# The second expert stage's front taken apart: its lists built in the attention's last steps, its late groups judged inside the expert loop

## The reference

```python
x = x + 0.5 * ffn(layernorm(x))      # stage 1
x = x + attention(layernorm(x))      # 16 heads of 64, causal, rotary
x = x + 0.5 * ffn(layernorm(x))      # stage 2, the same weights

def ffn(x):                          # per token, 8 experts, the best 2
    logits = x @ router.T            # 8 values
    top_vals, top_idx = top_k(logits, 2);  shares = softmax(top_vals)
    out = sum over the two e of  share_e * ( (silu(x @ gate[e].T) * (x @ up[e].T)) @ down[e].T )
```

## Time and profile before

| | us |
|---|---|
| runs shown (3): lowest, median, highest | 1264.59, 1265.62, 1267.65 |
| the profiled execution, its own time | 1263.21 |
| its span, first to last instruction | 1261.5 |
| TensorE busy (matmuls) | 1196.3, 95% |
| VectorE busy | 905.5, 72% |
| ScalarE busy | 791.4, 63% |
| GpSimd busy | 814.1, 65% |

### The profile page before, as it was taken

How to read it: one execution, slowest core, us unless ns; L and a number is a source line. 1 busy time by engine, 2 the same in 40 slices (tenths; PEclk the granted TensorE clock), 3 DMA queues, 4 the chain that set the end, 5 groups by cost and what they waited for, 6 DMA issues and landing times. The chain is left out here.

```text
span 1261.5 us, 28429 instructions
## 1 busy us (share of the span) xinstructions
PE 1196.3 (95%) x8838; PEld 912.5 (72%) x8838; DVE 905.5 (72%) x1995; ACT 791.4 (63%) x2264; POOL 814.1 (65%) x888
## 2 busy tenths in 40 slices
PE   7799999979999999999999999999999879999992
PEld 6588888856667666666667667766666668888881
DVE  6775344468888888888888997798998767533543
ACT  4665665656667666667667667767666656555552
POOL 4233356259888788788787787677666437666662
PEclk8899999989999999999999999999999969999996
DMA  9135122122221222122212222211221051113223
GB/s 323 32 96 155 57 56 70 42 69 56 62 53 42 60 60 50 44 60 54 57 46 51 62 64 51 60 43 43 52 49 37 18 184 43 47 50 113 62 63 110
DMA packets 87758, 86.54 MB, mean 69 GB/s; under 512 B 11248, under 2 KB 78704, under 8 KB 87232
## 3 DMA queue, kind: packets, MB, share of 16 engines
q1 hardware_dynamic: 76640, 65.50, 20.1%
q0 software_dynamic: 8864, 18.17, 5.2%
q10 hardware_dynamic: 2112, 1.05, 0.3%
HBM read 33.43 MB, written 17.69 MB: 41 GB/s over the span
## 5 line engine op out<-in xcount | busy, mean ns | idle before, releaser
L1915 POOL TENSOR_SCALAR at_prob<-at_prob,at_rec 128x128 f32<-128x128 f32 (+3 forms) x256 | 311.8, 1223 | 154.2 <-DVE at_rec L2126 152.3
L2306 ACT ACTIVATE at_prob<-at_s,at_nb 128x128 f32<-128x128 f32 (+3 forms) x512 | 264.7, 535 | 16.8 <-DVE at_nb L2118 13.4
L2317 ACT ACTIVATE at_probT<-at_pt 128x128 f32<-128x128 f32 (+3 forms) x256 | 105.2, 437 | 223.5 <-PE at_pt L2022 223.1
L790 POOL DMA_INDIRECT f_xb<-xn_dram,f_source x142 | 141.2, 994 | 160.4 <-PE f_b L1285 100.3
L2118 DVE TENSOR_REDUCE at_nb<-at_s 128x2 f32<-128x256 f32 (+3 forms) x256 | 203.5, 816 | 7.8 <-PE at_s L2008 7.8
L1447 DVE TENSOR_TENSOR f_hid<-f_b,f_silu 128x512 f32<-128x512 f32 x142 | 98.5, 693 | 135.8 <-PE f_b L1298 99.6
L2022 PE MATMUL at_pt<-ident,at_prob 128*128 128x128 f32 x1280 | 183.1, 275 | 5.5 <-DVE at_probT L2140 1.6
L2112 DVE TENSOR_TENSOR at_turned<-at_pj,rope 128x1024 f32<-128x1024 f32 x122 | 148.9, 1220 | 44.7 <-PE at_pj L1969 41.7
L2003 PE MATMUL at_s<-at_KT,at_QT 64*128 64x128 f32 (+3 forms) x1024 | 175.2, 460 | 5.2 <-DMA at_KT<-at_probT 2.8
L1909 POOL TENSOR_TENSOR at_R<-at_turned 128x512 f32<-128x512 f32 x126 | 157.4, 1268 | 24.0 <-DVE at_turned L2112 24.0
L2022 PEld LDWEIGHTS at_pt<-ident,at_prob 128*128 128x128 f32 x1280 | 140.9, 141 | 26.9 <-issue 15.5
(11 more groups left out here) (326 smaller groups left out, 2220.1 us busy)
## 6 DMA issues: line engine op xcount, KB each, us to landing
at_QT<-at_R SPq DMA_DIRECT2D x128, 128.0 KB, 2.4
at_KT<-at_R SPq DMA_DIRECT2D x124, 128.0 KB, 2.4
ys_dram<-y SPq DMA_DIRECT2D x71, 64.0 KB, 1.7
f_down<-down_t SPq DMA_DIRECT2D x2, 2048.0 KB, 9.3
xn_dram<-f_xn SPq DMA_DIRECT2D x12, 256.0 KB, 6.7
f_xb<-xn_dram,f_source POOLq DMA_INDIRECT x142, 2.5
X<-x SPq DMA_DIRECT2D x4, 512.0 KB, 6.2
gate<-gate_t SPq DMA_DIRECT2D x8, 256.0 KB, 5.1
```

What stands on the lines that cost most here:

```text
L790: pool.indirect_dma_start(out=xb[j % AHEAD][:, :], out_offset=None, in_=xn_dram, in_offset=bass.IndirectOffsetOnAxis(ap=routing.source[:, ...
L1915: pool.tensor_scalar(w, w, rec[:, q, 1:2], None, ALU.mult).then_inc(probB_ready, 1)
L2306: act.activation(prob[q][:, h, :], s_bank[q % 2][:, h, 0:n], ACT.Exp, bias=nb[:, q, h:h + 1], scale=1.0, accum_out=sums[:, q, h:h + 1]).th ...
L2317: act.activation(probT[0][:, 0:q + 1, q * P:(q + 1) * P], pt_bank[0][:, at:at + (q + 1) * P].rearrange("p (b r) -> p b r", r=P), ACT.Copy) ...
```

## The change

`Lead` gets the tiles for the leading lists (`place_lists`) in the space of `w_hi` and `w_lo`, and the four gather buffers with them. The attention's steps then build the leading lists: `blocked` at the end of VectorE's step 61, two `spots` each at the end of steps 62 and 63, `numbered` on GpSimd behind its step 62, `token_numbered` at the end of ScalarE's steps 62 and 63, `find` in TensorE's step 64 between `out_project` and the last `turn_probs`, `take_found` and `sources` at the end of VectorE's step 64. GpSimd issues the first four gathers behind its last step, in the attention's block. The front's block is gone. Its loads and stores stand at the head of the loop's block on SP, up and down first; groups 4 to 6 are normalised at the head of the loop and turned and judged in step 0 ahead of `project(0)`; the last group is normalised in step 0 and turned and judged in steps 2 to 4; its factors come from VectorE alone, without the square root, in step 0. `targets` of the leading part moves to step 1, and the late tiles' sorting starts at step 4 instead of 0 and ends at 22 instead of 20.

```diff
@@ Lead @@
+        self.routing.place_lists(room)
+        self.xb = [room(f"xb{k}", [P, P]) for k in range(self.AHEAD)]
...
+    def gather(self, pool, j):
+        routing, sure = self.routing, self.routing.sure
+        pool.wait_ge(routing.lists_ready, routing.SOURCES[j >= sure])
+        if j in (0, sure):
+            pool.wait_ge(self.xn_out, 16 * (self.NB // 4 if j else self.LEAD // 4))
...
@@ ffn @@
-            if lead is not None:
-                LATE_GROUPS = range(LEAD_GROUPS, GROUPS)
-                with nc.Block() as block:
...
-        COUNT_AT = 3
-        FIND_AT = 12
+        CHOOSE_AT, COUNT_AT, PLACE_AT, DIGITS_AT, FIND_AT = (4, 7, 10, 10, 14) if lead else (0, 3, 6, 7, 12)
+        BLOCKED_AT = DIGITS_AT + 1
+        SPOTS_AT = BLOCKED_AT + 2
...
@@ ffn, sync @@
+                    sp.dma_start(up[1][:, :, :].bitcast(F32), up_lo_dram).then_inc(up_lo_moved, 16)
+                    sp.dma_start(down[:, :, :, :], down_t).then_inc(down_in, 16)
+                    for g in LATE_GROUPS:
+                        sp.wait_ge(xn_ready, g + 1)
+                        if g < LAST:
+                            sp.wait_ge(xn_ready_pool, g - LEAD_GROUPS + 1)
+                        sp.dma_start(xn_dram[4 * g * P:4 * (g + 1) * P, :].rearrange("(n p) d -> p n d", p=P),
+                                     late_xn[:, 4 * g - LEAD:4 * g + 4 - LEAD, :]).then_inc(xn_out, 16)
...
@@ ffn, gpsimd @@
-                for j in range(AHEAD):
-                    gather(pool, j)
+                if lead:
+                    for g in range(LEAD_GROUPS, LAST):
+                        for n in (4 * g + 2, 4 * g + 3):
+                            one = pool.tensor_scalar(late_xn[:, n - LEAD, :], X[:, n, :], rstd[:, n:n + 1],
+                                                     lead.shift[:, n:n + 1], ALU.mult, ALU.add)
+                        one.then_inc(xn_ready_pool, 1)
...
@@ ffn, tensor @@
-                    if SPLITS and j == 0:
-                        pe.wait_ge(w_lo_dve, 4)
+                    if j == 0:
+                        if SPLITS:
+                            pe.wait_ge(w_lo_dve, 4)
+                        else:
+                            pe.wait_ge(up_lo_moved, 16)
...
+                        if lead and j == 0:
+                            late_turn(LEAD_GROUPS)
+                            late_turn(LEAD_GROUPS + 1)
+                            late_judge(LEAD_GROUPS)
+                            late_turn(LEAD_GROUPS + 2)
+                            late_judge(LEAD_GROUPS + 1)
+                            late_judge(LEAD_GROUPS + 2)
                         if has(j, -2):
                             turn_hidden(j - 2, k)
+                        if lead and j in LAST_TURNED:
+                            last_turn(j)
+                        if lead and j in LAST_JUDGED:
+                            last_judge(j)
...
@@ ffn, scalar @@
                 routing.odds(act, 0, exp_ready)
+                if lead:
+                    late_normed(LEAD_GROUPS)
+                    late_normed(LEAD_GROUPS + 1)
                 for j in range(-1, BLOCKS + 3):
+                    if lead and j == 0:
+                        late_taken(LEAD_GROUPS)
+                        late_normed(LEAD_GROUPS + 2)
+                        late_taken(LEAD_GROUPS + 1)
+                        late_taken(LEAD_GROUPS + 2)
...
                     step(act, j, j % AHEAD)
+                    if lead and j == 0:
+                        late_normed(LAST)
...
@@ ffn, vector @@
-                    routing.targets(dve, 0)
+                    for n in range(NB - 4, NB):
+                        dve.bn_stats(stats[:, n, :], X[:, n, :]).then_inc(moments.stats_ready, 1)
...
                 for j in range(-1, BLOCKS + 3):
+                    if lead and j == 0:
+                        some = slice(NB - 4, NB)
+                        dve.wait_ge(moments.stats_ready, NB)
+                        variances(link, dve, some, stats, mean, rstd, tmpa, tmpb)
+                        guess(link, dve, some, mean, rstd, tmpa)
+                        for _ in range(3):
+                            refine(link, dve, some, rstd, tmpa, tmpb)
...
@@ attention @@
+        LEAD_BLOCKED = STEPS - 3
+        LEAD_FOUND = STEPS
+        found_bank = s_bank[0][:, 0, 0:2 * routing.most]
...
@@ attention, gpsimd @@
                         normalise_b(i, 2)
+                    if i == LEAD_BLOCKED + 1:
+                        for k in range(2):
+                            routing.numbered(pool, 0, k, lead.lead_numbered)
+                for j in range(lead.AHEAD):
+                    lead.gather(pool, j)
...
@@ attention, tensor @@
                         out_project(i - 2)
+                    if i == LEAD_FOUND:
+                        pe.wait_ge(exp_ready, 8 * STEPS)
+                        pe.wait_ge(lead.lead_numbered, 2)
+                        for c in range(4):
+                            routing.find(pe, 0, c, found_bank)
...
@@ attention, vector, lead_last @@
+                    if i == LEAD_BLOCKED:
+                        routing.blocked(dve, 0, 0)
+                        routing.blocked(dve, 0, 1)
+                    if i in (LEAD_BLOCKED + 1, LEAD_BLOCKED + 2):
+                        for c in range(2):
+                            routing.spots(dve, 0, 2 * (i - LEAD_BLOCKED - 1) + c)
+                    if i == LEAD_FOUND:
+                        routing.take_found(dve, 0, found_bank)
+                        routing.sources(dve, 0)
                     if i == REST_FACTORS:
                         lead.halves(dve, 1)
...
@@ attention, scalar @@
-                act.activation(lead.tmpb[:, 0:1], lead.tmpa[:, 0:1], ACT.Sqrt)
+                    if i in (LEAD_BLOCKED + 1, LEAD_BLOCKED + 2):
+                        routing.token_numbered(act, 0, i - LEAD_BLOCKED - 1)
```

More of the change, by code:

```diff
@@ L340, in open, with place_later @@
         self.spot = sb("spot", [P, BLOCKS])
[L341 removed]
+    def place_later(self, sb):
+        self.counts = sb("counts", [P, 2, self.E * self.n[1]])
+        self.past = sb("past", [P, (self.blocks - self.sure + 6) * 3 * self.E])
     def hits_of(self, dve, r, k, logits):
@@ L637, in pack, with __init__, __call__ @@
                 one.then_inc(self.lists_ready, 1)
+class Room:
+    def __init__(self, nc, name, first, stop):
+        self.nc, self.name, self.first, self.stop = nc, name, first, stop
+    def __call__(self, name, shape, dt=F32):
+        size = math.prod(shape[1:]) * (2 if dt == BF16 else 4)
+        tile = self.nc.alloc_sbuf_tensor_at(f"{self.name}_{name}", shape, dt, offset=self.first)
+        self.first += -(-size // 32) * 32
+        assert self.first <= self.stop
+        return tile
 class Lead:
-    def __init__(self, nc, ctx, X, xn_dram, router_t, ident, stats, mean, rstd, tmpa, tmpb, wts, const, NB, E):
+    AHEAD = 4
+    def __init__(self, nc, ctx, X, xn_dram, router_t, ident, stats, mean, rstd, tmpa, tmpb, wts, const, NB, E, room):
         def sem(n):
@@ L1105, in ffn @@
         gate_bank, up_bank, hid_bank, x_bank, y_bank = bank[0:2], bank[2:4], bank[4:6], bank[6], bank[7]
+        if lead:
+            LATE_GROUPS = range(LEAD_GROUPS, GROUPS)
+            LAST = GROUPS - 1
+            late_xn = sb("late_xn", [P, NB - LEAD, P], ctx=work)
+            late_xts = [sb(f"late_xts{k}", [P, 512], ctx=work) for k in range(2)]
+            late_logits = hid_bank[1][:, 0:(NB - 4 - LEAD) * E]
+            last_xts = late_xts[LAST % 2]
+            last_logits = x_bank[:, 2 * P:2 * P + 4 * E]
+            late_turned, late_judged = lead.xt_psum, lead.lg_psum
+            LAST_TURNED = {2: range(0, 3), 3: range(3, 4)}
+            LAST_JUDGED = {3: range(0, 3), 4: range(3, 4)}
         xt_psum = sem("xt_psum2")
@@ L1261, in gather_back @@
                     ).then_inc(odd_in if b else first_in[m // 2], 16)
-                for j in range(AHEAD):
-                    gather(pool, j)
+                if lead:
+                    for g in range(LEAD_GROUPS, LAST):
[3 more added lines that the diff above has]
+                        one.then_inc(xn_ready_pool, 1)
+                else:
+                    for j in range(AHEAD):
+                        gather(pool, j)
                 for j in range(BLOCKS + 3):
```

242 lines of the change are left out of this document (115 added, 127 removed).

## The result

The changed kernel takes 1271.78 us (median; 1267.63 to 1272.7) where the kernel before takes 1265.37 (1264.59 to 1267.65): a ratio of 1.0042, 95% interval 1.0029 to 1.0056. It is slower, by more than the noise, and outside the forecast range (1259.8 to 1270.2). The profiled execution took 1271.77 us with a span of 1270.0, 8.5 us above the span of before.

A forecast was written before the change was run, and what follows sets the result against it. TensorE was taken to bound the kernel, so only its waits, lower clock or reduced work pay. Head −10.35, attention's tail +8.6 and loop +1.4 summed to −0.35: 1265.3 us for the median, range 1259.8 to 1270.2.

The forecast's parts named there:

- head: From the block's start to project(0): 19.55 us become 9.2, −10.35; up's landing gives the lower bound, 8.6.
- (a): End of VectorE's step 61: two block rows, 2 × 0.80 us, against 0.85 idle: +0.75.
- (b): End of VectorE's step 62: two spot tiles, 2 × 1.22 us, against 1.29 idle: +1.15.
- (c): End of VectorE's step 63: two more spot tiles, 2.44 us against no idle, delaying what queues behind: +2.4.
- (d, g): find's 32 matmuls between out_project(62) and the last turn, +1.5, and TensorE's clock falling at find, +1.1.
- (e): Attention's end: source list and four gathers, 6.0 us, against the old chain's 5.94; block ends with the later: +0.3.
- (f): Two GpSimd products beside VectorE delay the normalisation before a maximum of step 63: +1.4, bounds 0 and 3.05.
- loop: TensorE, never idle there, pays for the last group's four transposes and 8 judging matmuls: +1.4.
- exclusive lock: Rival: inserts wait for GpSimd normalisations begun before them, both products come between VectorE's instructions: +5.0, 1270.3 us; chance 0.08.
- up waits for down: Rival at project(0): up lands only when down has too, after 14.3 us: +5.4, 1270.7 us; chance 0.1.

The follow-up runs named there:

- The two runs on the gathers: Against the changed kernel: all four gathers moved into the loop's block, 1267.51 us; only gather 0 left at the attention's end, 1268.04 us.
- the run with the extra turns: Changed kernel plus unread turns of the identity in TensorE's waits in step 63 and ahead of out_project(62): 1267.37 us, ratio 1.0005.
- the second traces of both kernels: Both kernels run again untouched for another trace each: the changed one 1270.35 us, the one before 1265.22 us.

## Why the prediction was wrong

Term by term, forecast and measured:

| term | forecast | measured |
|---|---|---|
| head | −10.35 | −9.98 |
| (a) blocked, step 61 | +0.75 | +0.73 |
| (b) spots, step 62 | +1.15 | +1.34 |
| (c) spots, step 63 | +2.4 | +2.39 |
| (d, g) find, and the clock at it | +2.6 | +2.72 |
| (e) lists and gathers against the old end | +0.3 | +4.46 |
| (f) products beside VectorE | +1.4 | +1.82 |
| clock in step 63 | none | +1.45 |
| loop | +1.4 | −0.6 |
| ahead of the change | none | +4.15 |

(a) is the 0.92 of the table above less 0.19, which the attention lost between the two maxima and which two traces of before differ by as well (0.17). (b) and (f) share 3.16: the two held operations took 1.19 and 1.15, and 0.17 and 0.35 in the kernel before, which makes 1.82; the rest is put down to the spots.

**The failed step is (e): "The block ends with the later: +0.3".** The forecast let the attention's block end when the last gather instruction had ended, and laid the hand-over of an ordinary block behind it. The two runs on the gathers show a block's end that waits 4.3 to 4.6 us behind GpSimd's last gather, and that is gone when the gather stands elsewhere. The trace of before had a row for it that I did not look for, since I looked only at the ends of the attention and of the front, where GpSimd had nothing in flight: at the end of the expert loop the last scatter ends at 1239.65, and the next block's first load stands at 1244.49, 4.84 us later. With that row (e) would have been +4.6. What the sentence says of the engines did come true: the last gather ended at 1026.58, 0.41 behind the residual's end at 1026.17. The block just does not end there.

**(f) and the clock in step 63** are one mis-sized mechanism with a tail. The price was within its bounds (0 to 3.05), but what was held up were not normalisations: it was two operations of 0.17 us each, until the end of the product beside them. I read the first pair of the earlier trace rows as a VectorE operation that takes twice as long; by the two operations here it is rather one that waits. The Trainium skill (SBUF — State Buffer, section "SBUF: two separate sides") has whoever starts first, a GpSimd operation or a VectorE operation of certain kinds, hold the shared pair for its whole instruction. For a GpSimd product with two inputs the run with the products on VectorE agrees (1.19 becomes 0.16). For GpSimd's normalisation with one input the changed kernel agrees no more than the second pair of the earlier trace rows: begun at 996.24, it was drawn out to 2.52 by spot tiles that began after it. So the rival "exclusive lock" was half right, and the doubt that I drew from one pair was good for that kind of instruction only. Spot tiles and hold together left TensorE without work from 1000 to 1002, and its clock fell there a first time, which the forecast had only at find; the run with the extra turns shows 1.56 for it. The hold alone is not to blame: with the products on VectorE the clock falls there too.

**The loss ahead of the change** was no term, because nothing there was edited. It comes and goes: by 1.4 us between two traces of the kernel before, by 3.6 between traces of the changed kernel's code. The 4.15 are those of two single traces, of which the one before was quick (1263.21 against a median of 1265.37); of the 6.41 us between the medians the rests explain 4.4 to 4.5, which leaves about 2 for it. Without it the sum would be +4.4 against the forecast −0.35: inside the range, but still off by (e).

**What held:** the head, its bound by up's landing (project(0) waited 0.37 us for it), and its lower clock; that down comes forward at no price (the rival "up waits for down" is out: up landed after 9.3 us with down right behind it); the sizes of (a) to (d). In the second traces of both kernels the head measures −10.65 (19.49 us become 8.84, with up landed after 8.1). **The loop** was dearer in its first steps, as forecast, by less: block 4's first gate product stands 0.78 later after project(0) than before, and 0.84 in the second traces. The rest of the −0.6 comes later: 0.3 less along the steps, in both pairs of traces, and 1.1 less behind the last block's first gate product (28.91 against 29.98 us). This last belongs to the execution and not to the change: in the second traces it is 29.87 against 30.03, and the loop in all +0.4. No pair comes near the forecast +1.4.

**Slips in the sums.** In (e), 6.0 against 5.94 makes +0.06 and not +0.3; 4.2 MB at the rate of the earlier trace rows take 14.0 us and not 14.3; and the +1.4 of (f) is given without a working. None of them decides the result.

## What to carry to other kernels

At the end of a block, look at what GpSimd issued last: behind an indirect transfer the next block started 4.3 to 4.8 us after it here, whatever the other engines did, so such transfers belong at a place where the block goes on. Work that fills an engine in a chain of short waits has two prices, its own length and the clock of a TensorE that it leaves idle; the same work in gaps of that engine cost 0.4 us behind the maximum of step 63 here, where it had cost 6.6. And before a difference of traces is read, take the time of a mark ahead of the edit: two traces of one program can differ there by more than the edit is worth.

## What was not expected of the hardware

- Behind GpSimd's indirect transfers the next block starts late: 4.57 us after four gathers, 4.33 after one, 4.84 after the scatters at the loop's end of before; 0.52 behind the residual with none. The rows of these gathers had been moved 3.3 to 3.5 us before the next block's start.
- Rows gathered beside the loads of up and down were there 9.28 and 9.39 us into the block, whether they were issued 1.14 or 2.88 us into it; alone a gather lands in 2.5. Up's own landing was within 0.3 us of that in four traces, and 1.4 us earlier in another.
- A VectorE operation of 0.17 us beside a two-input GpSimd product ends when the product ends, 0.02 us later in both pairs.
- After the same wait at the attention's start, TensorE's full clock came back by 280 us in one trace and not by 285 in another.
